# Magnitudes of two weights on VectorE, earlier and finer steps ahead of the first group, in a graph network kernel

## The chip, the core and the metric

The kernel runs on one core of one Trainium2 chip. A core has five engines with queues of their own: TensorE (PE in the profile, its weight loads PEld), VectorE (DVE), ScalarE (ACT), GpSimd (POOL) and SyncE (SP), which here only starts DMAs. They meet at semaphores: an instruction waits until a counter has a value, and its finished predecessor has raised it. The metric is the device time of one execution in microseconds; lower is better.

## The reference, cut to what matters

`x` is 64 x 128 x 512 (batch, channel, node). Everything is float32.

```python
def reference(x, adj, bias, W_lang, W_grav, W_V, W_O, gate_logit, log_sigma):
    # layer 0, over the 512 nodes, one graph for the whole batch
    xn = transpose(x, (2, 0, 1))                              # node, batch, channel
    x_norm = xn / maximum(norm(xn, axis=-1), 1e-12)
    mean_sim = einsum('nbl,mbl->nm', x_norm, x_norm) / B      # 512 x 512
    A = the 153 largest of each row of mean_sim without its own node, else 0
    dinv = where(A.sum(0) > 0, rsqrt(A.sum(0)), 0)
    An = dinv[:, None] * A * dinv[None, :]
    x = layernorm(x + transpose(einsum('sd,sbl->dbl', An, xn @ adj) + bias))
    # layer 1, a causal graph over the 128 channels of each batch item
    z_l, z_g, v = x @ W_lang.T, x @ W_grav.T, x @ W_V.T
    K_l = rows of max(cos(z_l, z_l), 0), causal, no diagonal, sum 1
    K_g = rows of exp(-dist2(z_g, z_g) / (2 sigma^2)), causal, no diagonal, sum 1
    K = w * K_l + (1 - w) * K_g                               # w = sigmoid(gate_logit)
    return layernorm(x + (K @ v) @ W_O.T)
```

## The kernel before

A float32 product is made of float16 parts: each operand is split into a high part (a cast) and a low part (the operand less its high part), and `three` (lines 263 to 267) multiplies high by high, high by low and low by high. So most tiles take a cast on ACT (a function named ..._high) and a subtraction on POOL or DVE (..._low). To keep the parts in range, each matrix is first scaled by a power of two from its largest magnitude, which the kernel reads from sums of squares.

The program has a prologue and a loop. The prologue takes about the first 190 us:

1. **Similarities.** `x` comes in 16 chunks (`NC`) of 4 rows (`CL`) each. For every chunk ACT squares, DVE sums and normalises (line 1445), ACT casts (L1009), POOL subtracts (L409, one instruction for each of the 4 rows, which raises `xn_l_ready`), and PE adds rows 0 and 1 of the 512 x 512 similarity matrix (`rows_01`, which waits for that row's `xn_l_ready`). After the last chunk PE makes rows 2 and 3 from the kept parts (`gram`), while the other engines work on rows 0 and 1.
2. **Magnitudes.** ACT squares the four weights and `adj` with a sum (L1048, L1072, L1074) into columns of `magn`. PE turns `magn` after chunk 4 of `gram`, DVE takes the maximum of each, ACT its root, PE spreads it after chunk 6 (L621), and DVE makes the scales (`scales`), which release ACT's scaling of the weights (L1085).
3. **The 153 nearest.** `pick` runs on DVE, for node rows 0 and 1 (pair 0) and then 2 and 3 (pair 1). It takes mean and deviation of a row (the root is ACT's, `deviation`), counts over three guessed thresholds, and takes the rest by maxima. Its count goes to PE (`needs_along`, L609), and its results (`keep`, L1640) are summed on PE (`degrees`, L909).
4. **Weight products.** Beside `pick`, PE multiplies W_V by W_O (`vo_product`), the first group's x by adj (`first_project`), and turns the other two weights (`turn_weight`, L644, with banks freed by ACT's `turned_low`, L1139) and multiplies each with itself (`upper_product`).
5. **The scaled graph** (L1701 to L1719) and **the first group**: `mix_nodes`, layernorm, `project_z`, and `project_group(1)`, which multiplies the second group's x by adj, into banks 0 to 3 that the z products before it have to leave first.

The loop then takes 16 groups of 4 batch items. Nothing in its body is changed; only the call for group 0 (in which the second group's x is projected) is.

Each engine runs its queue in the order in which the code is written, and the order was written by hand. Most tiles lie in one large SBUF tile, `arena`, so rows are told apart by their lines. Two more names: `first_x` is the first group's x, loaded when POOL has made the first low part (`w_l_ready` 1), and `xg[1]` is the second group's x.

## Time and profile before

| | us |
|---|---|
| median of 3 runs | 940.64 (940.01 to 943.67) |
| the profiled execution's own time | 940.67 |
| its span, first to last instruction | 938.90 |
| PE busy | 915.7 (98%) |
| DVE busy | 750.0 (80%) |
| ACT busy | 538.4 (57%) |
| POOL busy | 304.1 (32%) |

The profile lists every instruction of one execution with its start and length. In a timeline row stand the start, the time taken (of several merged instructions together), the engine, the line, the operation, out<-in, the shapes and the count, and in brackets how long the engine had been idle before it and what ended that. PE matmuls are pipelined, so starts are the better measure there. PEclk is the share of TensorE's full clock that was granted.

### The profile page before, as it was taken

How to read it: one execution, taken by the hardware profiler on the slowest of the kernel's cores; microseconds unless marked ns; L12 is line 12 of the kernel's file. 1: busy time of each engine (PE TensorE's matmuls, PEld its weight loads, DVE VectorE, ACT ScalarE, POOL GpSimd, SP SyncE). 2: the span in 40 equal slices, each digit the busy share in tenths (PEclk: the TensorE clock that was granted, in tenths of full speed). 3: DMA queues.
4: the chain of work that ended last, by engine and by line, in shares of the span. 5: the costliest groups of instructions: out<-in, count | busy, mean ns of one | idle time of the engine just before them, and what ended most of it. 6: DMA issues, size and time to landing. Idle time of an engine off the chain costs nothing.

```text
span 938.9 us, 18940 instructions
## 1 busy us (share of the span) xinstructions
PE 915.7 (98%) x6856; PEld 539.8 (57%) x6856; DVE 750.0 (80%) x1720; ACT 538.4 (57%) x984; POOL 304.1 (32%) x420
## 2 busy tenths in 40 slices
PE   8999998999999999999999999999999999999995
PEld 6777876565555464646464646454545454556452
DVE  5887588778887888888888888888888888887767
ACT  6987676676373646464646464646464646463623
POOL 5888262045050505050505050505050505050500
PEclk9999999999999999999999999999999999999998
DMA  8554121102323131313131313232323232321211
GB/s 307 190 196 148 60 91 45 46 2 44 103 49 100 37 109 37 108 37 108 38 108 38 107 38 107 39 106 39 106 39 106 40 105 40 107 43 59 45 46 45
DMA packets 100792, 75.58 MB, mean 80 GB/s; under 512 B 79504, under 2 KB 79632, under 8 KB 98832
## 3 DMA queue, kind: packets, MB, share of 16 engines
q1 hardware_dynamic: 100752, 75.05, 27.9%
q8 instruction: 24, 0.39, 0.2%
q14 instruction: 16, 0.13, 0.0%
HBM read 38.86 MB, written 16.78 MB: 59 GB/s over the span
## 4 chain that ended last, share of the span: by engine, by line
PE 63%; DVE 14%; ACT 4%; issue 3%; DMA 1%; POOL 1%; DVEq 0%; SPq 0%; ACTq 0%; POOLq 0%
PE bank L265 13%; PE bank L267 12%; PE bank L266 12%; PE pair L265 7%; PE pair L267 7%; PE pair L266 7%; DVE arena L1813 4%; DVE arena L1803 2%; DVE arena L1478 1%; ACT arena L1107 1%; PE bank L790 1%; ACT arena L1245 1%; PE bank L752 1%; PE bank L751 1%; DVE stats L1792 1%
## 5 line engine op out<-in xcount | busy, mean ns | idle before, releaser
L265 PE MATMUL bank<-arena 128*128 128x512 f16 (+2 forms) x1056 | 292.2, 301 | 4.1 <-DVE arena L1813 2.0
L266 PE MATMUL bank<-arena 128*128 128x512 f16 (+2 forms) x1056 | 291.8, 300 | 0.0
L267 PE MATMUL bank<-arena 128*128 128x512 f16 (+2 forms) x1056 | 291.8, 300 | 0.0
L265 PE MATMUL pair<-arena 128*128 128x512 f16 (+1 forms) x400 | 150.7, 377 | 0.0
L266 PE MATMUL pair<-arena 128*128 128x512 f16 (+1 forms) x400 | 150.4, 376 | 0.0
L267 PE MATMUL pair<-arena 128*128 128x512 f16 (+1 forms) x400 | 150.3, 376 | 0.0
L265 PEld LDWEIGHTS bank<-arena 128*128 128x128 f16 x1056 | 103.2, 98 | 66.0 <-DVE arena L1813 4.3
L267 PEld LDWEIGHTS bank<-arena 128*128 128x128 f16 x1056 | 103.3, 98 | 62.9
L266 PEld LDWEIGHTS bank<-arena 128*128 128x128 f16 x1056 | 103.3, 98 | 55.0 <-issue 0.7
L460 POOL TENSOR_TENSOR sq_parts<-cf,zero 128x4 bf16<-128x4 f32 x15 | 3.1, 208 | 373.9 <-DVE cf L1865 373.9
L1245 ACT ACTIVATE arena<-bank 128x512 f16<-128x512 f32 x64 | 37.5, 588 | 95.5 <-PE bank L267 95.5
L445 POOL TENSOR_TENSOR arena<-arena 128x512 f16<-128x512 f32 x60 | 69.4, 1156 | 54.8 <-ACT arena L1240 52.8
L441 POOL TENSOR_TENSOR arena<-arena 128x512 f32<-128x512 f32 x60 | 76.0, 1267 | 29.5 <-ACT arena L1122 29.0
L409 POOL TENSOR_TENSOR arena<-arena 128x512 f16<-128x512 f32 x64 | 72.8, 1160 | 21.0 <-ACT arena L1009 20.9
L267 PEld LDWEIGHTS pair<-arena 128*128 128x128 f16 x400 | 39.1, 98 | 46.3
L1813 DVE SCALAR_TENSOR_TENSOR arena<-bank,arena 128x512 f16<-128x512 f32 x64 | 43.9, 686 | 27.0 <-ACT arena L1245 27.0
L265 PEld LDWEIGHTS pair<-arena 128*128 128x128 f16 x400 | 39.0, 98 | 44.9
L266 PEld LDWEIGHTS pair<-arena 128*128 128x128 f16 x400 | 39.1, 98 | 42.4
L1235 ACT ACTIVATE arena<-arena,ln 128x512 f32<-128x512 f32 x64 | 51.3, 805 | 18.1 <-DVE ln L1782 18.1
L1250 ACT ACTIVATE arena<-bank 128x512 f16<-128x512 f32 x32 | 19.1, 596 | 68.6 <-PE bank L267 68.6
L1478 DVE SCALAR_TENSOR_TENSOR arena<-arena,up 128x512 f16<-128x512 f32 x60 | 43.8, 773 | 18.0 <-ACT arena L1107 18.0
L417 POOL TENSOR_TENSOR arena<-arena 128x256 f16<-128x256 f32 x45 | 30.9, 722 | 73.7 <-ACT arena L1153 34.1
(383 smaller groups left out, 1951.3 us busy)
## 6 DMA issues: line engine op xcount, KB each, us to landing
arena<-in_x SPq DMA_DIRECT2D x32, 1024.0 KB, 5.6
out_dram<-arena SPq DMA_DIRECT2D x15, 1024.0 KB, 4.3
arena<-arena SPq DMA_TRANSPOSE x74, 3.2
arena<-in_x SPq DMA_DIRECT2D x2, 512.0 KB, 4.5
arena<-in_w_grav_t SPq DMA_DIRECT2D x1, 1024.0 KB, 7.3
arena<-in_w_lang_t SPq DMA_DIRECT2D x1, 1024.0 KB, 5.4
arena<-in_w_v SPq DMA_DIRECT2D x1, 1024.0 KB, 8.4
arena<-in_w_o_t SPq DMA_DIRECT2D x1, 1024.0 KB, 9.3
```

The source lines that it names most:

```text
L265: pe.matmul(dst, ah, bh, start=start, stop=False)
L266: pe.matmul(dst, ah, bl, start=False, stop=False)
L267: return pe.matmul(dst, al, bh, start=False, stop=stop)
L409: pool.tensor_tensor(xn_l[:, c * CL + t, :], xc[c % SLOTS][:, t, :], xn_h[:, c * CL + t, :], ALU.subtract).then_inc(s["xn_l_ready"], 1)
L417: last = pool.tensor_tensor(dst[:, mine, :], raw[:, mine, :], hi[:, mine, :], ALU.subtract)
L441: pool.tensor_tensor(y[:, b, :], y[:, b, :], xg[slot][:, b, :], ALU.add).then_inc(s["y_ready"], 1)
L445: pool.tensor_tensor(h_l[:, b, :], h[slot][:, b, :], h_h[:, b, :], ALU.subtract).then_inc(s["hl_ready"], 1)
L1235: act.activation(h[slot][:, b, :], y[:, b, :], ACT.Identity, scale=ln1[:, 3, b:b + 1], bias=ln1[:, 4, b:b + 1]).then_inc(s["h_ready"], 1)
L1245: act.activation(z_h[i][:, E_ORDER[n], :, :], bank[n][:].rearrange("p (b n) -> p b n", b=GB), ACT.Copy, scale=U_DOWN).then_inc(done, 1)
L1250: act.activation(half_h[i], bank[4 + i][:].rearrange("p (b n) -> p b n", b=GB), ACT.Copy, scale=HALF_DOWN).then_inc(done, 1)
L1478: low = dve.scalar_tensor_tensor(x_l[:, b, :], xg[slot][:, b, :], up[:, 5:6], x_h[:, b, :], ALU.mult, ALU.subtract)
L1813: dve.scalar_tensor_tensor(z_l[i][:, e, :, :], bank[n][:].rearrange("p (b n) -> p b n", b=GB), U_DOWN, z_h[i][:, e, :, :], ALU.mult, ALU.s ...
```

## The change

- **Magnitudes.** ACT squares only weights 1 and 2; weights 0 and 3 are squared by DVE, with one multiply-and-sum instruction each, between the last normalisation and the filling of `work`. `adj` is squared right after the first two rows of S. PE turns `magn` after chunk 3 instead of 4 and spreads the roots after chunk 5 instead of 6.
- **Pair 0 of `pick`.** Each row is filled and its statistics are taken at once, instead of both rows first.
- **Rows 2 and 3 on PE.** Chunk 0 of `gram` is parted in two around `finish_diagonal(0)` and `(1)`. In the last chunk row 2 is finished ahead of row 3. `finish_diagonal(2)`, `(3)` and the turn of S go ahead of most of `turn_weight(1, 0)`, and ACT's `turned_high(1, 0)` goes behind S.
- **Finer subtractions.** POOL's low parts of weights 2 and 3, of the first x and of its product are made in pieces of 128 instead of 256.
- **Roots.** `deviation(1)` moves on ACT from behind `vo_out(0)` to behind the scaling of `first_x`; the degrees' root moves ahead of `upper_out(1, 2)`. On PE `needs_along(1)` goes into the middle of `vo_product(3)`, and the second half of `degrees` ahead of `upper_product(1, 2)`.
- **The second group's x.** Its cast and subtraction are made earlier, and PE projects it into banks 4 to 7.

```diff
+        squares_v = at(184 * KIB, [KB, NODES])
...
-                low(blocks(vo_l[i]), blocks(w_raw[2 + i]), blocks(vo_h[i]), 8, s["w_l_ready"])
+                low(blocks(vo_l[i]), blocks(w_raw[2 + i]), blocks(vo_h[i]), 16, s["w_l_ready"])
...
-            low(blocks(first_x_l), blocks(first_x), blocks(first_x_h), 8, s["x_l_ready"])
+            low(blocks(first_x_l), blocks(first_x), blocks(first_x_h), 16, s["x_l_ready"])
...
-                low(xw_l[:, b, :, :], first_xw[:, b, :, :], xw_h[:, b, :, :], 2, s["xw_l_ready"])
+                low(xw_l[:, b, :, :], first_xw[:, b, :, :], xw_h[:, b, :, :], KB, s["xw_l_ready"])
...
-            gram(0, range(2, KB), first=True)
+            gram(0, range(2, KB), first=True, ts=range(0, 2))
             finish_diagonal(0)
             finish_diagonal(1)
+            gram(0, range(2, KB), ts=range(2, CL))
...
-                gram(c, range(2, KB), last=(c == NC - 1))
-                if c == 4:
-                    pe.wait_ge(s["magn_ready"], 5)
-                    pe.wait_ge(s["magn_x"], 1)
+                if c < NC - 1:
+                    gram(c, range(2, KB))
+                else:
+                    gram(c, range(2, 3), last=True)
+                    gram(c, range(3, KB), last=True)
+                if c == 3:
+                    pe.wait_ge(s["magn_ready"], 3)
+                    pe.wait_ge(s["magn_x"], 3)
                     pe.transpose(bank[4][0:8, 0:P], magn[:], ident[:]).then_inc(s["magn_all_ready"], 1)
-                if c == 6:
+                if c == 5:
...
-            turn_weight(1, 0)
             finish_diagonal(2)
             finish_diagonal(3)
-            turn_weight(1, 1)
+            turn_weight(1, 0, range(0, 2))
             pe.wait_ge(s["S_ready"], 6)
             turn(bank[7][:, P:2 * P], 2, 3).then_inc(s["S_turned"], 1)
+            turn_weight(1, 0, range(2, KB))
+            turn_weight(1, 1)
...
-            def project_group(g):
+            def project_ahead(g):
                 pe.wait_ge(s["x_l_ready"], g + 1)
-                for b in range(GB):
-                    wait(pe, s["zg_l_ready"], g * GB - GB + (b + 1))
-                    project_x(g, b, x_h, x_l)
-
-            def project_ahead(g):
-
-                pe.wait_ge(s["x_l_ready"], g + 1)
-                pe.wait_ge(s["k_ready"], g - 1)
+                wait(pe, s["k_ready"], g - 1)
+                if isinstance(g, int) and g == 1:
+                    pe.wait_ge(s["u_out"], 2 * (2 * KB - 1))
...
-                    project_group(g + 1)
+                    project_ahead(g + 1)
...
-            vo_product(3)
+            vo_product(3, range(0, HALF))
             needs_along(1)
+            vo_product(3, range(HALF, KB))
             for b in range(GB):
                 first_project(b)
-            for d in range(KB):
-                upper_product(1, d)
+            upper_product(1, 0)
+            upper_product(1, 1)
             degrees(range(2, KB))
+            upper_product(1, 2)
+            upper_product(1, 3)
...
-            for n, i in enumerate((1, 0, 3)):
+            for n, i in enumerate((1, 2)):
                 act.wait_ge(s[f"w_in{i}"], 16)
                 wait(act, s["magn_ready"], n)
                 act.activation(squares, w_raw[i], ACT.Square, accum_out=magn[:, i:i + 1]).then_inc(s["magn_ready"], 1)
...
-            turned_high(1, 0)
...
+            turned_high(1, 0)
             turned_high(1, 1)
             act.wait_ge(s["w_in2"], 32)
             act.activation(first_x, first_x, ACT.Copy, scale=up[:, 5:6]).then_inc(s["w_scaled"], 1)
+            deviation(1)
...
             vo_out(0)
-            deviation(1)
...
+            x_high(1, 1, 1, range(0, 1))
             turned_low(0, 2)
             turned_low(0, 3)
+            x_high(1, 1, 1, range(1, HALF))
             first_roots(0, 0)
             first_norm(0, 0, 0)
             first_norm(0, 0, 1)
+            x_high(1, 1, 1, range(HALF, GB))
...
             upper_high(0)
-            x_high(1, 1, 1, range(GB))
...
             dve.tensor_reduce(magn[:, 5:6], chunk_max[:], AX.X, ALU.max).then_inc(s["magn_x"], 1)
+            dve.wait_ge(s["consts_made"], 4)
+            for n, i in enumerate((0, 3)):
+                dve.wait_ge(s[f"w_in{i}"], 16)
+                dve.wait_ge(s["magn_x"], n + 1)
+                dve.scalar_tensor_tensor(squares_v, w_raw[i], 1.0, w_raw[i], ALU.mult, ALU.mult,
+                                         accum_out=magn[:, i:i + 1]).then_inc(s["magn_x"], 1)
+            dve.wait_ge(s["magn_x"], 3)
             dve.wait_ge(s["xn_l_ready"], NC * CL)
             dve.memset(work[:, :, NODES:], PAD).then_inc(s["work_ready"], 1)
...
             for b in range(GB):
                 hT_low(b)
+            x_low(1, 1, range(GB))
```

What this makes of the queues is shown at three places. A row is an instruction with its line (the lines of the changed kernel lie a few further on), its operation, out<-in, the size of the output, what it waits for, and a count.

On DVE, at the end of the similarities, before:

```order
L1463 TENSOR_REDUCE magn<-chunk_max 128x1 [waits nrm_in]
L1465 MEMSET arena 128x4x8 [waits xn_l_ready]
L1470 COPY arena<-arena 128x512 [waits S_ready,consts_made]
L1472 TENSOR_TENSOR arena<-arena,self_mark 128x128 [waits work_ready]
L1470 COPY arena<-arena 128x512 [waits S_ready]
```

and now:

```order
L1470 TENSOR_REDUCE magn<-chunk_max 128x1 [waits nrm_in]
L1475 SCALAR_TENSOR_TENSOR arena,magn<-arena 128x2048 [waits magn_x,w_in0,consts_made]
L1475 SCALAR_TENSOR_TENSOR arena,magn<-arena 128x2048 [waits magn_x,w_in3]
L1479 MEMSET arena 128x4x8 [waits xn_l_ready,magn_x]
L1484 COPY arena<-arena 128x512 [waits S_ready,consts_made]
L1486 TENSOR_TENSOR arena<-arena,self_mark 128x128 [waits work_ready]
L1521 BN_STATS row_stats<-arena 128x6
```

Two instructions over 2048 elements each stand between the last reduction and the memset, and the statistics of row 0 stand ahead of the second copy.

On ACT, around the scaling of the first group's x (L1175, now L1178) and the root for pair 1 of `pick` (L1059, now L1067), before:

```order
L1135 ACTIVATE arena<-bank 128x512 [waits wn_ps]
L1175 ACTIVATE arena<-arena,up 128x2048 [waits w_in2]
L1178 ACTIVATE arena<-arena 128x2048 [waits w_l_ready,w_scaled]
L1139 ACTIVATE arena<-bank 128x512 [waits wn_rest] x2
L1157 ACTIVATE arena<-bank 128x512 [waits vo_ps]
L1159 ACTIVATE arena,vo_magn<-arena 128x512 [waits vo_out]
L1059 ACTIVATE guess<-guess 128x2 [waits var_ready]
```

and now:

```order
L1138 ACTIVATE arena<-bank 128x512 [waits wn_ps] x2
L1178 ACTIVATE arena<-arena,up 128x2048 [waits w_in2]
L1067 ACTIVATE guess<-guess 128x2 [waits var_ready]
L1182 ACTIVATE arena<-arena 128x2048 [waits w_l_ready,w_scaled]
L1142 ACTIVATE arena<-bank 128x512 [waits wn_rest] x2
L1160 ACTIVATE arena<-bank 128x512 [waits vo_ps]
```

The root stands four large instructions earlier, and the cast of the first x and `turned_low` (L1139, now L1142) stand behind it.

On ACT ahead of the first group, where `x_high` of the second group (L1107, now L1110) stood behind the last weight product's parts (L1153), before:

```order
L1153 ACTIVATE arena<-arena 128x1280 [waits u_out]
L1107 ACTIVATE arena<-arena,up 128x512 [waits xw_ps,x_in1]
L1107 ACTIVATE arena<-arena,up 128x512 x3
L1396 ACTIVATE arena<-arena,vo_scale 128x2048 [waits vo_steps]
L1245 ACTIVATE arena<-bank 128x512 [waits zg_ps] x2
```

and now:

```order
L1110 ACTIVATE arena<-arena,up 128x512 [waits xw_ps,x_in1]
L1142 ACTIVATE arena<-bank 128x512 [waits wn_rest] x2
L1110 ACTIVATE arena<-arena,up 128x512 [waits xw_ps,x_in1]
L1233 ACTIVATE ln<-ln 128x2 [waits ln1_var]
L1235 ACTIVATE ln<-ln 128x2 [waits ln1_log]
L1240 ACTIVATE arena<-arena,ln 128x512 [waits ln1_ready] x2
L1110 ACTIVATE arena<-arena,up 128x512 [waits xw_ps,x_in1]
L1110 ACTIVATE arena<-arena,up 128x512
```

The four casts are spread over the steps of the first layernorm, some 20 instructions earlier in the queue.

## Rows read from the trace of the kernel before

**Rows 1.** The page: busy time of each engine, its share, its instructions.

```profile
PE 915.7 (98%) x6856; PEld 539.8 (57%) x6856; DVE 750.0 (80%) x1720; ACT 538.4 (57%) x984; POOL 304.1 (32%) x420
```

**Rows 2.** Busy time by stretch: length, each engine's busy time, PEclk, DMA share, GB/s.

```profile
80.00:100.00 20.00, 20.00 (x162) 14.31 (x161) 11.82 (x21) 14.88 (x17) 17.36 (x16) 1.00 0.45 159
160.00:180.00 20.00, 18.73 (x96) 10.40 (x95) 16.97 (x47) 11.40 (x20) 0.00 (x0) 0.91 0.13 48
180.00:200.00 20.00, 18.73 (x149) 12.10 (x148) 13.74 (x31) 17.83 (x33) 5.00 (x6) 1.00 0.16 54
240.00:939.00 699.00, 684.67 (x4915) 374.13 (x4913) 565.73 (x1289) 366.88 (x711) 182.17 (x266) 0.99 0.26 68
```

**Rows 3.** Timeline of PE, the starts behind its waits in the prologue.

```profile
146.74 0.38 PE L609 MATMUL bank<-ident,guess 128*1 128x128 f32 x2 [0.82 <-DVE guess L1568]
...
157.36 1.95 PE L909 MATMUL bank<-ones,arena 128*128 128x1 f32 x16 [1.04 <-DVE arena L1640]
...
164.13 2.02 PE L644 MATMUL bank<-arena 128*128 128x128 f32 x16 [0.72 <-ACT arena L1139]
166.71 0.38 PE L265 MATMUL bank<-arena 128*128 128x512 f16 x1 [0.56 <-DVE arena L1719]
...
194.19 0.22 PE L265 MATMUL bank<-adj_h,arena 128*128 128x128 f16 x1 [1.26 <-DVE arena L1813]
```

**Rows 4.** Busy time by stretches of 2 us, columns as above.

```profile
156.00:158.00 2.00, 0.96 (x12) 0.78 (x9) 1.87 (x3) 1.44 (x3) 0.00 (x0) 1.00 0.00 0
...
160.00:162.00 2.00, 2.00 (x14) 2.00 (x13) 1.06 (x5) 0.85 (x2) 0.00 (x0) 0.63 0.96 362
162.00:164.00 2.00, 1.41 (x5) 0.40 (x3) 1.26 (x5) 2.00 (x4) 0.00 (x0) 0.52 0.28 106
```

**Rows 5.** Timeline of DVE at the end of the similarities.

```profile
92.70 2.35 DVE L1445 SCALAR_TENSOR_TENSOR arena<-arena,bank 128x1024 f32<-128x1024 f32 x2 [1.89 <-PE bank L513]
94.97 0.16 DVE L1463 TENSOR_REDUCE magn<-chunk_max 128x1 f32<-128x16 f32 x1
99.72 0.09 DVE L1465 MEMSET arena<- 128x32 f32 x1 [4.59 <-POOL arena L409]
```

**Rows 6.** Timeline of POOL, the low parts.

```profile
95.15 4.50 POOL L409 TENSOR_TENSOR arena<-arena 128x512 f16<-128x512 f32 x4 [0.37 <-ACT arena L1009]
...
118.71 11.09 POOL L417 TENSOR_TENSOR arena<-arena 128x256 f16<-128x256 f32 x16 [19.05 <-ACT arena L1087]
129.76 0.42 POOL L427 TENSOR_TENSOR adj_l<-adj_sb,adj_h 128x128 f16<-128x128 f32 x1
136.03 5.08 POOL L417 TENSOR_TENSOR arena<-arena 128x256 f16<-128x256 f32 x8 [5.84 <-ACT arena L1178]
...
188.35 4.54 POOL L417 TENSOR_TENSOR arena<-arena 128x256 f16<-128x256 f32 x5 [34.12 <-ACT arena L1153]
```

**Rows 7.** DVE groups by shape, 182 to 200 us: count, busy us, mean ns, idle before.

```profile
L1478 DVE SCALAR_TENSOR_TENSOR arena<-arena,up 128x512 f16<-128x512 f32 x4 | 4.4, 1168 | 2.6 <-ACT arena L1107 2.6
...
L1486 DVE SCALAR_TENSOR_TENSOR arena<-bank,arena 128x512 f16<-128x512 f32 x2 | 1.3, 682 | 0.0
```

**Rows 8.** Timeline of PE, the start of the last row of the last chunk.

```profile
99.71 0.23 PE L519 MATMUL bank<-arena 128*128 128x128 f16 x1
```

**Rows 9.** Timeline of ACT around the diagonal blocks and the first group's x.

```profile
102.19 0.42 ACT L1040 ACTIVATE rinv_rep<-bank 128x128 f32<-128x128 f32 x2
...
131.94 2.01 ACT L1175 ACTIVATE arena<-arena,up 128x2048 f32<-128x2048 f32 x1
134.04 1.91 ACT L1178 ACTIVATE arena<-arena 128x2048 f16<-128x2048 f32 x1
135.85 1.06 ACT L1139 ACTIVATE arena<-bank 128x512 f16<-128x512 f32 x2
```

**Rows 10.** Timeline of DVE, two waits in the chain of the nearest nodes.

```profile
113.99 0.17 DVE L1658 TENSOR_SCALAR pw<-bank 128x8 int32<-128x8 int32 x1 [0.40 <-PE bank L621]
...
138.29 0.32 DVE L1531 SCALAR_TENSOR_TENSOR guess<-guess 128x2 f32<-128x2 f32 x1 [2.14 <-ACT guess L1059]
```

More of the change, by code:

```diff
@@ L634, in project_x, with turn_weight @@
                 mm.then_inc(s["xw_ps"], 1)
-            def turn_weight(i, j):
+            def turn_weight(i, j, ks=range(KB)):
                 n = (1 - i) * KB + j
@@ L642, in turn_weight @@
                 wait(pe, s["wn_out"], n - 1)
-                for k in range(KB):
+                for k in ks:
                     mm = pe.matmul(bank[4 + j % 2][:, k * P:(k + 1) * P], w_raw[i][:, k, j * P:(j + 1) * P],
                                    ident_w[i], start=(k == 0), stop=(k == KB - 1), skip_group_check=True)
-                mm.then_inc(s["wn_ps"], 1)
-            turn_weight(1, 0)
+                if ks[-1] == KB - 1:
+                    mm.then_inc(s["wn_ps"], 1)
             finish_diagonal(2)
             finish_diagonal(3)
-            turn_weight(1, 1)
+            turn_weight(1, 0, range(0, 2))
             pe.wait_ge(s["S_ready"], 6)
             turn(bank[7][:, P:2 * P], 2, 3).then_inc(s["S_turned"], 1)
+            turn_weight(1, 0, range(2, KB))
+            turn_weight(1, 1)
             def first_project(b):
@@ L662, in _, with vo_product @@
             OUT_OF_ROW = [2, 4, 6, 7]
-            def vo_product(d):
+            def vo_product(d, fs=range(KB)):
                 pe.wait_ge(s["w_l_ready"], 2)
@@ L667, in vo_product @@
                     pe.wait_ge(s["S_ready"], 8)
-                for f in range(KB):
+                for f in fs:
                     mm = three(pe, bank[d][:], vo_h[0][:, f, d * P:(d + 1) * P], vo_l[0][:, f, d * P:(d + 1) * P],
                                vo_h[1][:, f, :], vo_l[1][:, f, :], start=(f == 0), stop=(f == KB - 1))
-                mm.then_inc(s["vo_ps"], 1)
+                if fs[-1] == KB - 1:
+                    mm.then_inc(s["vo_ps"], 1)
             def less_high(i, j):
@@ L819, in body @@
                 if isinstance(g, int) and g == 0:
-                    project_group(g + 1)
+                    project_ahead(g + 1)
                     pe.wait_ge(s["w_l_ready"], 4)
-                    project_z(g, slot, 0, (s["xw_l_ready"], g * GB + GB), s["zl_ps"])
-                else:
-                    project_z(g, slot, 0, (s["zg_l_ready"], g * GB), s["zl_ps"])
+                project_z(g, slot, 0, (s["zg_l_ready"], g * GB), s["zl_ps"])
                 pe.wait_ge(s["zg_l_ready"], g * GB + GB)
@@ L1051, in _ @@
             cross_out(1)
-            act.wait_ge(s["magn_ready"], 3)
+            act.wait_ge(s["magn_ready"], 2)
             act.wait_ge(s["xn_l_ready"], NC * CL)
@@ L1056, in _ @@
             s_out(S[:, 1, P:], bank[1][:, 0:NODES - P])
+            act.activation(squares2[:, 0, 0:P], adj_sb[:], ACT.Square,
+                           accum_out=magn[:, 4:5]).then_inc(s["magn_ready"], 1)
+            act.wait_ge(s["magn_x"], 3)
             def deviation(pair):
@@ L1070, in _ @@
             fill_out(work[:, 3, 0:2 * P], bank[6][:, 0:2 * P])
-            act.wait_ge(s["w_in2"], 16)
-            act.activation(squares2, w_raw[2], ACT.Square, accum_out=magn[:, 2:3]).then_inc(s["magn_ready"], 1)
-            act.wait_ge(s["magn_ready"], 4)
-            act.activation(squares2[:, 0, 0:P], adj_sb[:], ACT.Square,
-                           accum_out=magn[:, 4:5]).then_inc(s["magn_ready"], 1)
             deviation(0)
@@ L1200, in _ @@
             x_biased(slice(0, HALF))
-            for d in range(KB):
-                upper_out(1, d)
-            x_biased(slice(HALF, GB))
+            upper_out(1, 0)
+            upper_out(1, 1)
             act.wait_ge(s["deg_in"], 1)
             act.activation(deg_t[:], deg_m[:], ACT.Sqrt).then_inc(s["roots_made"], 1)
+            upper_out(1, 2)
+            upper_out(1, 3)
+            x_biased(slice(HALF, GB))
             turned_high(0, 0)
@@ L1260, in body @@
                 if not has_previous:
-                    xw_high(g + 1, 0)
+                    xw_high(g + 1, 4)
                 if isinstance(g, int) and g == 0:
@@ L1499, in pick @@
                 g = lambda i: guess[:, i, :]
-                if pair == 0:
-                    dve.wait_ge(s["work_ready"], 5)
-                else:
+                if pair == 1:
                     dve.wait_ge(s["work_23_ready"], 6)
@@ L1506, in pick @@
                 for t in range(2):
+                    if pair == 0:
+                        fill_work(t, 2 + t)
                     dve.bn_stats(row_stats[:, t, :], S[:, r0 + t, :]).then_inc(ps, 1)
@@ L1533, in pick @@
                 n += 2
+                dve.wait_ge(s["work_ready"], 5)
                 for i in range(COUNTS):
@@ L1643, in _ @@
             dve.wait_ge(s["consts_made"], 4)
-            fill_work(0, 2)
-            fill_work(1, 3)
             ss = s["scale_steps"]
@@ L1842, in body @@
                 if not has_previous:
-                    xw_low(g + 1, 0)
+                    xw_low(g + 1, 4)
                 if has_second and has_previous:
@@ L2114, in _ @@
             dve.wait_ge(cs, 10)
-            x_low(1, 1, range(GB))
             body(0, 0, True, False)
```

## The prediction

> **What bounds the kernel now.** I read the busy shares first: PE is busy for 98% of the span, 915.7 of 938.9 us [rows 1], so it is PE's queue that time has to leave, or enter. Next the stretches: from 240 us on PE is busy for 684.67 of 699 us [rows 2], and nothing in that loop is changed. So the change can win only what PE idles in the prologue, and lose whatever it makes PE wait there. Third, the starts on PE that follow a wait, up to 200 us [rows 3]: 0.82 us for the count of pair 1 (L609), 1.04 for the last kept rows (L909), 0.72 for a freed bank (L644), 0.56 for the scaled graph (L265 behind L1719), 1.26 for the second group's x. These sum to 4.4 us; with the pipeline's tail, which these rows count as busy, each gap between two matmuls is some 0.2 us wider, say 5.4 in all. Last the clock: 1.00, but for 160 to 164 us, where 0.63 and 0.52 were granted [rows 4], so TensorE ran for about 3.4 us at the lower of its levels, 1.2 GHz. Ahead of that it had idled, and then run 16 matmuls one column wide in 1.95 us [rows 3].
>
> At the end of the similarities there is next to nothing to win: PE is busy for 20.00 of 20 us from 80 to 100 [rows 2]. What matters is who feeds it. POOL makes the last four low parts in 4.50 us from 95.15, 1.12 us each, without a pause [rows 6], the last ends at 99.65, and PE starts on it at 99.71 [rows 8]. POOL is the pace there, with no slack. DVE idles beside it from 95.13 to 99.72 [rows 5].
>
> **Squares on DVE: what they cost.** The two new instructions take 2048 elements each. L1445 takes 1.17 us for 1024 elements [rows 5], so one is 2.25 us and two are 4.5. On DVE alone they fit: they would end just before or a little behind 99.72, and DVE has nothing until S, 5 us later. But they read two operands from SBUF, as L1445 does not (its second comes from PSUM). What such an instruction does beside POOL is seen at 189 us: L1478, with both inputs in `arena`, takes 1168 ns, where L1486, of the same size but with one input in a bank, takes 682 [rows 7]. POOL pays at the same time: its five pieces there take 4.54 us, 0.91 each, against 5.08 for eight, 0.63 each, at 136 us [rows 6]. (4.54 - 5 x 0.63 = 1.4 us, for the two to three DVE instructions of 0.6 us that fell between.) So the engines take turns, an instruction of one, then one of the other, and each waits for the whole of the other's.
>
> Put at 95 us: POOL starts its first part at 95.15, just ahead of DVE, and ends at 96.27. DVE's first square runs to 98.45, POOL's second part to 99.55, DVE's second square to 101.8, POOL's third and fourth to 102.9 and 104.0. The last low part comes 4.3 us late. If DVE is first by a hair, the sum is the same. PE takes the four parts in steps of 1.04 us, so it waits 2.0 us for the second, 2.2 for the third, and starts the last at 104.0 in place of 99.7: **+4.3 us**, all on the path. From below, the cost is 0, if an instruction that reads the same tile twice does not meet POOL, or waits until POOL has finished. From above it is 4.5.
>
> The Trainium skill, "SBUF — State Buffer", section "Who interferes with whom", says that a DVE instruction with two SBUF inputs contends with a GpSimd one that reads SBUF, and that whoever starts first holds the shared port pair for the whole instruction. The trace agrees at 512 elements (1168 against 682 ns); that it holds over 2048 no row shows. By this rule the change loses here, as above.
>
> **The clock.** Between 97.6 and 102.9 us PE would have 1.04 us of work in 5.3. That is emptier than the stretch which came before the low clock at 160 us [rows 4]. I expect one period of 3.4 us at 1.2 GHz, as there, beginning some 4.4 us after the emptiness sets in (160.6 less 156.2), so at 102 and to 105.4. PE would have 2.5 us of it to work, and loses half: **+1.2 us**. Bounds: 0, and 3.4 for two full periods.
>
> **Magnitudes and pair 0.** ACT's three squares held up its copies of the diagonal blocks until 102.19 [rows 9]; without the third, and with chunk 0 parted, PE saves about 0.2 us. DVE gets the deviation of pair 0 some 0.8 us sooner (one row's statistics are taken while S is turned) and no longer waits 0.40 us for the spread roots [rows 10], so weights are scaled 1.2 us sooner. PE's turns of `magn` cost nothing, they only stand 1.6 us earlier. But then DVE waits for `needs_along(0)`, whose place on PE stays: of 1.2 us about 0.6 to 0.9 is left at the start of pair 1.
>
> **Finer subtractions.** 128 elements take 0.42 us alone (L427), 256 take 0.63, 512 take 1.12 [rows 6]; in a row I take 0.39. Sixteen are 6.2 us where eight were 5.08. DVE waits less for each; together POOL ends the two weights at about 131, 1.2 us later, and `vo_product(0)`, due at 130.9, waits some 0.3 us.
>
> **Roots, and the chain to the graph.** The deviation of pair 1 waited 2.14 us behind ACT's four instructions [rows 10]. Now ACT scales `first_x` until about 133.7, then stands until DVE has the variance at about 135.4 (136.15 before, less 0.75). DVE goes on at 135.7 in place of 138.29, **2.6 us sooner**, and with it the count and the kept rows. The price is on ACT: the cast of `first_x`, at 134.04 before, starts at 135.6, and `turned_low` ends its first tile at 138.1 in place of 136.4 [rows 9]. `turn_weight(1, 2)` needs that bank and is due at about 137.0: PE waits 1.0 to 1.3 us there, where it hardly waited. This takes the place of the 1.0 us at L609, which goes. The 1.2 us gap ahead of L909 goes too, since `degrees` finds its rows done at 155.3. DVE then gets the degrees at about 157.0 (159.34 before), but PE spreads the result only after both turns of weight 0, at 160.6 in place of 161.50. From there all is as before, at the higher clock: the graph's first tile, and with it `mix_nodes` (166.71), comes **1.15 us sooner** [rows 3]. Bounds: 0, if ACT's stand at the root grows by a microsecond, and 2.5, if it vanishes.
>
> **The second group's x.** Its four casts fall into idle stretches of ACT, and its low parts come before POOL begins the next ones. At 192.8 us PE goes straight on into banks 4 to 7: the gap ahead of 194.19 goes, 1.26 us in the row and 1.43 between matmuls [rows 3]: **-1.4 us**. What is next late, the parts of z for `project_z(0)`, is due 2.7 us later and done by then.
>
> **Sum.** +4.3 + 1.2 - 0.2 - 1.15 - 1.4 = +2.75 us. The profiled execution took 940.67, 0.03 from the median of 940.64, with 1.8 us around its span that nothing changes. 940.67 + 2.75 = **943.4 us**.
>
> **Rivals.**
> - *A: the squares cost nothing on POOL.* Then the clock's term goes too: -2.75, 937.9 us. For it: no row shows one tile read twice, nor 2048 elements. Against it: L1478 [rows 7].
> - *B: POOL is held up, but the clock stays at the higher level.* +4.3 - 2.75 = +1.55, 942.2 us. For it: PE idled for 1 us and more elsewhere (146, 194 us) with no lower clock. Against it: no such stretch there is as empty.
> - *C: the delay at the similarities brings two periods at 1.2 GHz, and ACT's stand at the root eats the gain on the graph.* It is still the squares that decide, with the low clock falling on full work: +4.3 + 3.4 - 1.6 = +6.1, 946.8 us. It decides from 3.2 us of clock loss on, with the rest as forecast.
> - *D: no hold-up, and the chain to the graph gains its upper bound:* -2.75 - 1.35 = -4.1, 936.5; faster by more than 0.5% only if the freed clock at 160 us also gives its whole microsecond back.
>
> **Chances.** Forecast 0.42, B 0.20, A 0.14, C 0.18, D 0.06. A measurement of this kernel can tell about 0.5%, 4.7 us, from no change: below 935.9 is faster, above 945.3 slower. That gives slower 0.20 (C and a little of the forecast's upper end), faster 0.06, the same 0.74. The forecast alone has 942 to 945. To hold 8 in 10 the range takes in A and the lower half of C: 937.5 to 946.0.
>
> **What would show it.** Right: the two DVE instructions at 95 to 102 us take well over 2.3 us each by the profile, or POOL's L409 there does; PE's last row starts near 104; PEclk falls below 1 within 100 to 106; DVE's wait for the root of pair 1 is under 0.4 us; PE waits about 1 us on L644 behind `turned_low` near 138 (all plus 4 to 5 us); no wait is left ahead of the second group's projection. Wrong, and then A: POOL's four parts still take 4.5 us and PE's last row starts by 100. The step most likely to fail is the hold-up, then the clock.

## The result, and the profile after

The changed kernel takes **945.51 us** (median of 8 executions, 943.95 to 949.37), the kernel before 940.85 in the same session (8, 940.01 to 943.67): ratio **1.005, 95% interval 1.0034 to 1.0066**, some 4.7 us slower. Run again later (*e12*), beside 23 executions of the kernel before, it took 944.57 us (6, 944.35 to 945.43) against 941.57, ratio 1.0038 [1.0026, 1.005]. Forecast were 943.4 us and a range of 937.5 to 946.0. In *e4*, *e9* and *e10* below one execution each took 1.3, 1.09 and 2.3 ms; the medians hold it, the ratios leave it out. The profiled execution took 944.26 us, 3.6 more than that of before. Line numbers are those of each kernel: L409 of before is L410 after, L417 is L418, L265 is L266, L644 is L650.

The page of the kernel after, its span and its busy row (PE 1.0 us busier than in [rows 1], in a span 3.6 us longer):

```profile
span 942.5 us, 18980 instructions
PE 916.7 (97%) x6856; PEld 540.0 (57%) x6856; DVE 753.3 (80%) x1724; ACT 535.0 (57%) x980; POOL 313.3 (33%) x452
```

The end of the similarities, timelines of POOL and of DVE, to be read against [rows 5, 6]:

```profile
95.27 8.59 POOL L410 TENSOR_TENSOR arena<-arena 128x512 f16<-128x512 f32 x4 [0.37 <-ACT arena L1014]
```

```profile
95.39 3.19 DVE L1475 SCALAR_TENSOR_TENSOR arena<-arena 128x2048 f32<-128x2048 f32 x1
...
98.69 3.05 DVE L1475 SCALAR_TENSOR_TENSOR arena<-arena 128x2048 f32<-128x2048 f32 x1
...
104.01 0.09 DVE L1479 MEMSET arena<- 128x32 f32 x1 [2.26 <-POOL arena L410]
```

POOL's four parts take 8.59 us where they took 4.50. Both squares are recorded with more than 3 us, where the same instructions take 2.29 us without POOL beside them (*e1* below). That fits a record which begins while the instruction still stands for its turn. The timeline of PE there, against [rows 8]:

```profile
97.60 0.27 PE L542 MATMUL bank<-arena 128*128 128x256 f16 x1
99.65 0.23 PE L520 MATMUL bank<-arena 128*128 128x128 f16 x1 [1.78 <-POOL arena L410]
...
100.59 0.27 PE L542 MATMUL bank<-arena 128*128 128x256 f16 x1
102.81 0.23 PE L520 MATMUL bank<-arena 128*128 128x128 f16 x1 [1.95 <-POOL arena L410]
```

The two waits show when POOL's second and third parts were done, just ahead of 99.65 and 102.81: 3.2 us apart, one part of 1.1 and one square of 2.2. These steps are those of engines that take turns by whole instructions. Busy time by stretches of 2 us (length, PE, PEld, DVE, ACT, POOL, then PEclk, DMA share, GB/s), first behind the waits, then at the place of [rows 4]:

```profile
101.00:103.00 2.00, 0.19 (x2) 0.17 (x3) 0.75 (x2) 0.00 (x0) 2.00 (x2) 1.00 0.00 0
103.00:105.00 2.00, 2.00 (x10) 1.09 (x8) 0.09 (x1) 0.00 (x0) 0.87 (x1) 0.52 0.00 0
105.00:107.00 2.00, 2.00 (x14) 1.27 (x13) 0.00 (x0) 0.52 (x2) 0.00 (x0) 0.63 0.00 0
```

```profile
160.00:162.00 2.00, 2.00 (x20) 1.84 (x18) 1.04 (x2) 1.15 (x5) 2.00 (x4) 1.00 0.00 0
162.00:164.00 2.00, 2.00 (x26) 1.86 (x27) 1.38 (x8) 0.62 (x3) 0.86 (x3) 1.00 0.79 236
```

The lower level (1.2 GHz) lay at 160 us before, and lies at 103 to 106.6 now, right behind the two waits. The starts on PE behind a wait from there on, against [rows 3], and the wait of DVE for the root of pair 1, against [rows 10]:

```profile
137.09 0.39 PE L266 MATMUL bank<-arena 128*128 128x512 f16 x1 [0.29 <-POOL arena L418]
...
143.60 0.57 PE L650 MATMUL bank<-arena 128*128 128x128 f32 x3 [0.73 <-ACT arena L1142]
...
168.48 2.02 PE L650 MATMUL bank<-arena 128*128 128x128 f32 x16 [1.34 <-ACT arena L1142]
...
240.22 0.39 PE L266 MATMUL bank<-arena 128*128 128x512 f16 x1 [0.56 <-DMA arena<-arena]
```

```profile
141.21 0.16 DVE L1545 SCALAR_TENSOR_TENSOR guess<-guess 128x2 f32<-128x2 f32 x1 [0.27 <-ACT guess L1067]
```

The waits at the count of pair 1, at the last kept rows and at the second group's x are gone, that at the start of `mix_nodes` is 0.14 us (0.56 before); one at L650 near 143 us and one for a transposing DMA at 240 us are new.

How much later than before each place is reached tells where the time went. PE's turns of S: +5.56 us. The start of `mix_nodes`: 170.64 for 166.71, +3.93. The second group's x: +2.50. What starts at 256 us before, in the third group: +3.52. The last instructions: +3.62.

### The profile page after: what moved, and what is told of

Read it like the earlier page. It is cut to its first block, busy times and chain, and to the rows that moved or that the text cites. A ratio compares the mean times of both kernels' runs of the same rounds, so it can differ in the third digit from the quotient of the medians.

```text
span 942.5 us, 18980 instructions
## 1 busy us (share of the span) xinstructions
PE 916.7 (97%) x6856; PEld 540.0 (57%) x6856; DVE 753.3 (80%) x1724; ACT 535.0 (57%) x980; POOL 313.3 (33%) x452
## 4 chain that ended last, share of the span: by engine, by line
PE 64%; DVE 13%; ACT 3%; issue 3%; DMA 1%; POOL 1%; SPq 1%; DVEq 0%; ACTq 0%; POOLq 0%
PE bank L266 13%; PE bank L268 12%; PE bank L267 12%; PE pair L266 7%; PE pair L268 7%; PE pair L267 7%; DVE arena L1825 4%; DVE arena L1815 2%; PE bank L794 1%; DVE arena L1492 1%; ACT arena L1110 1%; ACT arena L1250 1%; DMA arena<-arena 1%; PE bank L756 1%; PE bank L755 1%
## 5 line engine op out<-in xcount | busy, mean ns | idle before, releaser
L266 PE MATMUL bank<-arena 128*128 128x512 f16 (+2 forms) x1056 | 292.2, 300 | 4.9 <-DVE arena L1825 3.0
L266 PE MATMUL pair<-arena 128*128 128x512 f16 (+1 forms) x400 | 150.7, 377 | 0.0
L266 PEld LDWEIGHTS bank<-arena 128*128 128x128 f16 x1056 | 103.2, 98 | 67.3 <-DVE arena L1825 5.3
L446 POOL TENSOR_TENSOR arena<-arena 128x512 f16<-128x512 f32 x60 | 69.4, 1156 | 54.8 <-ACT arena L1245 52.8
L410 POOL TENSOR_TENSOR arena<-arena 128x512 f16<-128x512 f32 x64 | 76.9, 1224 | 21.1 <-ACT arena L1014 21.0
L266 PEld LDWEIGHTS pair<-arena 128*128 128x128 f16 x400 | 39.1, 98 | 44.8
L418 POOL TENSOR_TENSOR arena<-arena 128x128 f16<-128x128 f32 (+1 forms) x77 | 35.5, 497 | 66.9 <-ACT arena L1156 29.4
```

Of the source, the lines that this page charges most:

```text
L266: pe.matmul(dst, ah, bh, start=start, stop=False)
L410: pool.tensor_tensor(xn_l[:, c * CL + t, :], xc[c % SLOTS][:, t, :], xn_h[:, c * CL + t, :], ALU.subtract).then_inc(s["xn_l_ready"], 1)
L418: last = pool.tensor_tensor(dst[:, mine, :], raw[:, mine, :], hi[:, mine, :], ALU.subtract)
L446: pool.tensor_tensor(h_l[:, b, :], h[slot][:, b, :], h_h[:, b, :], ALU.subtract).then_inc(s["hl_ready"], 1)
```

## The experiments

Each has 5 to 12 executions and a ratio to the kernel before, run on the same chip in the same session. There were three sessions on three chips: *e1* to *e4*, *e5* to *e8*, *e9* to *e12*. Between two of them the ratios are the measure, not the medians.

One more number helps to read them, the mean granted clock of an execution. It holds the end of the program, where PE has nothing left to do and the lower level is granted in every profile, for 5 to 7 us:

```profile
936.00:942.00 6.00, 0.00 (x0) 0.00 (x0) 3.13 (x10) 1.84 (x4) 0.00 (x0) 0.50 0.46 175
```

A stretch of 3.4 us at half the clock takes another 0.0018 off the mean over 940 us. So it is in the fourteen profiles: 0.996 or 0.997 without such a stretch ahead of PE's last matmul, 0.994 or 0.995 with one, 0.993 with two or with one of 6.6 us.

**e3 and e4: the disputed cost alone.** The kernel before with two added DVE multiplies of 2048 elements, whose result nobody uses, where the change puts its squares; PE's turn of S waits for them. They differ in the second input alone.

```diff
+            for n, i in enumerate((0, 3)):
...
+                dve.scalar_tensor_tensor(squares_v, w_raw[i], 1.0, w_raw[i], ...)                  # e3
+                dve.scalar_tensor_tensor(squares_v, w_raw[i], 1.0, <bank 6, broadcast>, ...)       # e4
```

> The kernel before, with two added multiplies of 128x2048 on DVE that nothing uses, at the place of the new squares, both inputs from SBUF (a weight twice), and a wait of PE's turns of S on them. Theory: POOL's four L409 take 8.6 us, PE's last row starts at 104, a low clock follows, and the time is 940.85 + 4.3 + 1.2 = 946.3. Rival (any long DVE instruction there, or the waits, costs): the same for this run, but then the run with a PSUM operand must show it too.

> As the run before, but the second input of the two added multiplies is a bank of PSUM, repeated over the four blocks; the product is not used. Theory: DVE and POOL run side by side, 4.5 us for POOL's four parts, 940.8 to 941.1. Rival (length or the waits cost, not the second input): 945 or more. If DVE is slower with PSUM as an input, its two instructions end by 100.5 at the latest and nothing waits for them.

*e3*: 947.59 us, ratio 1.0073 [1.0058, 1.0088], 1.3 us more than forecast. *e4*: 941.36, 1.0005 [0.9994, 1.0015]. POOL and DVE in *e3*, then in *e4*:

```profile
95.19 8.59 POOL L410 TENSOR_TENSOR arena<-arena 128x512 f16<-128x512 f32 x4 [0.36 <-ACT arena L1011]
...
95.28 3.21 DVE L1469 SCALAR_TENSOR_TENSOR arena<-arena 128x2048 f32<-128x2048 f32 x1
```

```profile
95.15 4.52 POOL L410 TENSOR_TENSOR arena<-arena 128x512 f16<-128x512 f32 x4 [0.36 <-ACT arena L1011]
...
95.24 2.29 DVE L1469 SCALAR_TENSOR_TENSOR arena<-arena,bank 128x2048 f32<-128x2048 f32 x1
98.83 2.29 DVE L1469 SCALAR_TENSOR_TENSOR arena<-arena,bank 128x2048 f32<-128x2048 f32 x1 [1.30 <-DMA arena<-in_w_o_t]
```

Same place, same size, and the same starts (the second multiply stands for its weight's load and starts at 98.83 us here, at 98.75 in *e3*): with both inputs in SBUF, here one tile read twice, POOL loses 4.1 us and PE's turns of S come 5.5 us late; with one of them in a bank neither engine loses anything. This settles the mechanism. *e3* also shows a second stretch at 1.2 GHz, near where before has its own. It falls on fuller work: the start of `mix_nodes` is 6.2 us late, not 5.5. Stretches of *e3*, then of *e4*:

```profile
100.00:110.00 10.00, 8.05 (x71) 5.94 (x69) 1.74 (x2) 3.53 (x8) 3.79 (x2) 0.83 0.01 2
160.00:170.00 10.00, 8.30 (x61) 7.34 (x58) 5.80 (x21) 4.62 (x11) 0.00 (x0) 0.83 0.34 107
```

```profile
160.00:170.00 10.00, 8.25 (x52) 5.29 (x52) 8.73 (x22) 8.28 (x14) 0.00 (x0) 1.00 0.25 94
```

*e4* has the waits of before at the same places (0.83 us at 146.75, 1.05 at 157.38) and no low clock behind them; its `mix_nodes` starts 0.63 us sooner than before. So the stretch at 160 us belongs to the profiled execution and not to the kernel: of 87 further executions of the kernel before 33 have a mean of 0.996 or 0.997, which no profile with such a stretch has. Why it comes in some and not in others stays open.

**e1: the squares held back.** The changed kernel, with DVE's wait for POOL's last part ahead of the squares and not behind them.

```diff
             dve.wait_ge(s["consts_made"], 4)
+            dve.wait_ge(s["xn_l_ready"], NC * CL)
             for n, i in enumerate((0, 3)):
...
-            dve.wait_ge(s["xn_l_ready"], NC * CL)
```

> The changed kernel with one edit: DVE waits for POOL's last low part (xn_l_ready 64) before its two squares instead of behind them. Theory (two SBUF inputs hold POOL up): POOL's four parts are back at 4.5 us, PE starts its last row at 99.8, no low clock within 100 to 107 us, and the squares take 2.2 us each, so that they end at about 104.2 and the filling of work starts 0.3 us late. Time: 944.3 less 4.3 and 1.2 is 938.8, at most 939.3. Rival (the loss is elsewhere in the change, in the cast order or in the finer pieces): 944 or more, with the lines of POOL unchanged.

938.79 us (11, 937.21 to 940.62), ratio 0.9977 [0.9967, 0.9986]: one wait moved makes a kernel some 6 us faster than the changed one (0.9977 against 1.005 and 1.0038), and faster than the one before. The theory held. POOL's four parts take 4.51 us, the squares 2.29 each, PE has no wait there and no low clock at 103 us.

**e9: one square early, the other held back.** The changed kernel with DVE's wait for POOL's last part between the two squares.

> The changed kernel with its first square where the change put it, beside POOL's four subtractions, and only the second held back until POOL is done. Theory (POOL loses time in proportion to the time that DVE squares beside it: 4.1 us lost beside 6.2 us of squares in the changed kernel): one square of about 3.1 us costs POOL 2.0 us, POOL's parts take 6.5 us and not 8.6, PE waits about 2 us once, and without the second wait the low clock of 102 to 107 us does not come: 940.8 us. Rival (the low clock comes from any late row of chunks there): 942.

940.56 us, 0.9999 [0.9987, 1.0012]. POOL's four parts, and PE behind its one wait:

```profile
95.18 6.55 POOL L410 TENSOR_TENSOR arena<-arena 128x512 f16<-128x512 f32 x4 [0.37 <-ACT arena L1014]
```

```profile
99.55 0.23 PE L520 MATMUL bank<-arena 128*128 128x128 f16 x1 [1.77 <-POOL arena L410]
```

Half the squares, half the loss (2.05 of 4.1 us), and PEclk is 1.00 as long as PE works: one wait of 2 us did not bring the low clock, two within 5 us did, in *e3* as in both profiles of the changed kernel. The executions agree: 9 of 11 in *e9* have a mean clock of 0.996 or 0.997, none of the 14 of the changed kernel or the 5 of *e3* has. The theory held, the rival fell.

**e2 and e10: the magnitudes' part.** *e2* is the changed kernel with this part as before; *e10* the kernel before with this part alone and the squares held back.

> The changed kernel with the magnitudes as before: ACT squares all four weights at their old places, PE turns magn after chunk 4 and spreads the roots after chunk 6; the other edits stay. Theory: no hold-up, no low clock at 100 us; scales come 0.4 to 1.2 us later than in the run with late squares, which the chain of pair 1 feels by 0.3 to 0.8: 939.0 to 940.0. Rival: 944 or more.

> The kernel before with the magnitudes' part of the change alone (two weights squared by DVE, held back until POOL is done; magnitudes turned behind chunk 3 and 5), none of the other parts. Undoing this part in the changed kernel gave 941.6 us, against 938.8 with it and the squares held back. Theory (the part is worth something by itself, since ACT comes 1 to 2 us sooner to what DVE and PE wait for): 0.5 to 2 us faster than before, 939.5 to 940.5. Rival (it pays only together with the deviation taken sooner, which without it stands in front of ACT's other work): no difference, 941.

*e2*: 941.63, 1.0012 [0.9995, 1.003], 2.8 us above *e1* and above its own forecast; its executions are spread from 938.92 to 946.35. By the profiles, which both have a stretch at 1.2 GHz at 16 to 20 us, PE's last matmul comes 2.3 us later than in *e1*. *e10*: 941.54, 0.9996 [0.9984, 1.0007]: nothing, as its rival had it. In *e2* ACT squares until 103.8 us and PE waits 0.97 us for its copies of the diagonal blocks; DVE comes later to the variance of pair 1, and ACT, which since the change stands for it ahead of its other work, stands 3.03 us and not 1.67 (*e1*). In *e10* DVE waits 2.65 us for the root, which still lies behind ACT's other work:

```profile
138.68 0.31 DVE L1537 SCALAR_TENSOR_TENSOR guess<-guess 128x2 f32<-128x2 f32 x1 [2.65 <-ACT guess L1063]
```

Together they say: what DVE gains early is only passed on if the root is early too, and an early root is only cheap if DVE is early.

**e5 and e6: where ACT takes the deviation of pair 1**, both on *e1*.

```diff
-            deviation(1)
             act.wait_ge(s["w_scaled"], 3)
             act.wait_ge(s["w_l_ready"], 2)
             act.activation(first_x_h, first_x, ACT.Copy).then_inc(s["x_h_ready"], GB)
+            deviation(1)          # e5
             turned_low(1, 0)
             turned_low(1, 1)
             vo_out(0)
+            deviation(1)          # e6
```

> The kernel with the squares held back until POOL's last part (938.8 us, ratio 0.998 to the kernel before), and in it one more edit: ACT takes the second half's deviation behind the rounding of first_x and not ahead of it. In that kernel ACT stands 1.67 us for DVE's variance with the rounding, two halves of turned weights and the first vo product behind it, and PE waits 0.90 us at turn_weight(1, 2). Theory (ACT's stand is what PE waits for): the rounding fills the stand, ACT comes to the halves of the weights 1.5 us sooner, PE's 0.90 us wait goes, DVE goes on 0.2 us later, and the end comes 0.7 to 0.9 us sooner: about 938.0 us. Rival (the graph's chain decides, PE's wait costs nothing): the wait goes but comes back at the degrees or at mix_nodes, and the time stays at 938.8.

> The same kernel as the one before it, with the second half's deviation where the kernel before had it, behind the first vo product on ACT: DVE goes on about 2.4 us later (ACT at 139.4 and not at 136.9). Theory (the graph's chain is what the earlier deviation bought): the 0.90 us wait at turn_weight(1, 2) goes, but the waits at the needed rows (1.0 before) and at the degrees (1.2 before) come back, so the kernel is 0.5 to 1.2 us slower than with the deviation ahead: 939.3 to 940.0. Rival (the chain has slack of its own by now): no wait comes back, 0.9 us faster, 937.9.

*e5*: 940.21, 0.9986 [0.9976, 0.9997]. *e6*: 942.46, 1.0005 [0.9993, 1.0017], over 2 us above its theory's range. In *e5* the 0.90 us between matmuls at `turn_weight(1, 2)` goes and 1.07 us comes at the degrees (first row); in *e6* 1.54 us comes at the count (second fence) and 1.46 at the degrees, and with them, in the profiled execution, 6.6 us at 1.2 GHz from 158 us on:

```profile
155.16 1.95 PE L911 MATMUL bank<-ones,arena 128*128 128x1 f32 x16 [0.90 <-DVE arena L1655]
```

```profile
146.33 0.38 PE L611 MATMUL bank<-ident,guess 128*1 128x128 f32 x2 [1.37 <-DVE guess L1583]
```

So DVE's chain bounds here, and the wait at L650 only covers it: the rival of *e5* held. The root's new place is worth 2.6 us beside the other edits by the ratios (*e6* less *e1*; 3.7 by the medians of two chips), and part of it is clock. Four of the twelve executions of *e6* have a mean clock of 0.996 or 0.997; they take 939.99 to 940.65 us, where the five such ones of *e5* take 938.71 to 939.16. So the waits cost some 1.2 us against *e5*, and in the other eight a low clock comes on top.

**e7 and e8: the second x and the piece size undone**, both on *e1*.

> The kernel with the squares held back, and in it the second group's x undone: high and low parts at the end of the prologue, its product into banks 0 to 3 as these come free. Theory (the prediction's term of -1.4 us is right and stays to the end): PE waits 1.4 us again at the second group's x near 191 us, and everything behind is 1.4 us later: 940.2. Rival (part of it was given back at once: in the changed kernel 1.0 us of the gain went again at the second group's transposing DMA, which took 2.57 us and not 1.23): the end is only 0.4 us later, 939.2.

> The kernel with the squares held back, and in it POOL's subtractions in pieces of the size of before: 256 and 512 elements in place of 128. POOL's row took 0.39 us a piece of 128 and 0.63 us a piece of 256, so each of the two weights is done 1.2 us sooner. Theory (finer pieces are a cost): PE's 0.52 us wait for POOL at the first vo product goes, the end is 0.3 to 0.5 us sooner, about 938.4. Rival (finer pieces let DVE in sooner, and the graph's chain is late without them): DVE's selection ends later by some tenths, PE's waits at the degrees come back, and the time is 0.5 us or more longer, 939.3.

*e7*: 939.70, 0.998 [0.997, 0.9989]. The wait is back:

```profile
192.83 0.22 PE L266 MATMUL bank<-adj_h,arena 128*128 128x128 f16 x1 [1.26 <-DVE arena L1830]
```

Counted from the turns of S, *e7* stands 1.4 us behind *e1* at the second group's x, 1.9 at the third group and 1.3 at PE's last matmul. So the profiles have the term to the end; the executions can't tell it from the rival's 0.4, since the ratios are 0.0003 (0.3 us) apart and the medians 0.9 us, with overlapping intervals. *e8*: 940.86, 0.9993 [0.9981, 1.0004], 1.5 us above *e1* by the ratios, 2 by the medians, also with overlapping intervals. PE's wait for POOL is gone, but DVE's instructions beside POOL are longer, *e8* and then *e1*:

```profile
125.97 1.30 DVE L1635 TENSOR_SCALAR cut<-rank,guess 128x8 f32<-128x8 f32 x2
```

```profile
127.66 0.62 DVE L1635 TENSOR_SCALAR cut<-rank,guess 128x8 f32<-128x8 f32 x2
```

Without POOL beside them these two take 0.36 us. A piece of 256 makes each wait up to 0.63 us, one of 128 up to 0.39. Finer pieces cost POOL 2.7 us over both weights (13.82 for 11.09), yet counted from the turns of S the start of `mix_nodes` comes 0.9 us sooner with them, and PE's last matmul 1.3. So the rival held by the profile; by the executions it is likely, not shown.

**e11: the end of the chain in another order**, on *e1*.

```diff
+            <PE: wait for dinv, four transposes into bank 6>
             turn_weight(0, 0)
             turn_weight(0, 1)
-            <the same>
...
+            x_biased(slice(HALF, GB))
             upper_out(1, 2)
             upper_out(1, 3)
-            x_biased(slice(HALF, GB))
+            upper_high(1)
             turned_high(0, 0)
             turned_high(0, 1)
-            upper_high(1)
```

> The kernel with the squares held back (938.8 us), and in it the end of the graph's chain in another order: PE broadcasts the inverse roots right behind the upper products and ahead of two turned weights (which stood 1.8 us in front of it), ACT biases the second half of x in its idle time behind the degrees' root and takes the upper weight's high part ahead of the turned ones. Theory: DVE's scaling of the adjacency starts 1.7 us sooner, PE's wait of 1.52 us at turn_weight(0, 2) shrinks to about 0.9, mix_nodes starts 0.6 to 1.0 us sooner, and the end comes with it: 938.0. Rival (ACT's turned halves are late for the weights, since they have the upper part ahead of them): nothing gained, 938.8 or more.

**937.20 us** (6, 936.20 to 938.85), ratio **0.996 [0.9947, 0.9973]**, the fastest of all. The profiles of *e1* and *e11* are not in step (that of *e1* has a stretch at 1.2 GHz at 16 to 20 us), so dates are counted from PE's turns of S, at 106.52 and 104.81 us. DVE's scaling of the graph starts 57.76 us behind them in *e1* and 56.06 in *e11*, 1.70 sooner; `mix_nodes` 60.05 and 59.10, 0.95 sooner; the end 1.2 sooner. PE's 1.52 us ahead of `turn_weight(0, 2)` is 0.36, with 0.64 ahead of the second L684. By the profiles the theory held; the two ratio intervals, those of *e1* and *e11*, still overlap. Timeline of PE in *e11*:

```profile
158.34 0.66 PE L939 MATMUL bank<-ident,rinv_rep 128*128 128x128 f32 x4
...
162.05 2.02 PE L650 MATMUL bank<-arena 128*128 128x128 f32 x16 [0.19 <-ACT arena L1141]
```

**e12: the changed kernel again.**

> The changed kernel unchanged, beside the others on one chip, for the spread of its times: eight runs lay between 943.95 and 949.37 us, their mean granted clock between 0.995 and 0.991. Theory (each further stretch at the lower clock, as the kernel before has one at 160 us, costs 1.5 to 2.5 us, and the spread is nothing else): the times fall with the clock on the same steps, near 944 at 0.995 and near 946.5 at 0.993, and a run at 0.997 does not occur, since the stretch at 103 us is always there. Rival (the spread has another cause): times of one clock spread as far as all of them.

Its six times lie at 944.35 to 944.99 with a mean clock of 0.995 or 0.994 and at 945.43 with 0.993. In the first session 0.995 gave 943.95 to 944.33, 0.993 gave 945.45 to 946.70, 0.991 gave 949.23 and 949.37. No execution had more than 0.995. The theory held in the main: none reaches 0.996, and the times go by the clock, 0.994 with 0.995 (the end of the program makes that difference) and 0.993 above them, though in *e12* 1 us below the 946.5 forecast for it. By the profiles a step of 0.002 is one more stretch at 1.2 GHz. What it costs depends on what PE had to do in it: 1.6 us at 103 us (below), 0.6 at `mix_nodes` and 0.3 at the end for the one at 160 us (before against *e4*). Which stretches came in the slowest two no profile shows.

## Why the prediction was nearly right, and where not

The sum against the trace of the profiled execution, each term as the shift that appears at its place:

| term | predicted | measured |
|---|---|---|
| hold-up of POOL | +4.3 | +4.21, its last part done at 103.86 for 99.65 |
| the clock behind it | +1.2 | +1.59 |
| diagonal blocks | -0.2 | -0.24, so +5.56 at the turns of S |
| the graph's chain | -1.15 | -1.63 up to `mix_nodes` |
| second group's x | -1.4 | -1.43 |
| groups behind it | 0 | +1.12 |
| sum | +2.75 | +3.62 |

The diagonal blocks' term is read from *e8* and *e11*, which have neither hold-up nor an early low clock and whose turns of S start at 104.81 us (105.05 before); the clock is what is left of the 5.56. Two terms were too small by 1.5 us together (clock, groups), and the others erred by 0.65 the other way. That the forecast lies only 0.9 us from the profiled execution is in part luck. The first median of 945.51 lies past the 945.3 from which on the prediction called the result slower, with a chance of 0.20; that of *e12*, 944.57, does not.

- **Squares.** Right in each date: PE's waits 1.94 and 2.11 us between matmuls (2.0 and 2.2 forecast), DVE's second square done at 101.7 (101.8), PE's last row from 104.58 (104.0), since the clock was low by then. *e3* against *e4* shows the cause. Rival A is refuted. The trace agrees with the rule of the Trainium skill that the prediction weighed ("SBUF — State Buffer", "Who interferes with whom"), now at 2048 elements too, where no row of before showed it.
- **Clock.** Right in kind, one stretch of 3.4 us, 103.2 to 106.6 for 102 to 105.4, but under-sized: 1.59 us for 1.2. The prediction gave PE 2.5 us of work in the stretch; it began behind the second wait, so PE had work in all of it. *e9* removes one wait and the stretch with it: POOL's last part is done 2.08 us late (101.73), the turns of S are 1.83 late, and the difference is the diagonal blocks' gain, with no clock in it. Rival B is refuted for this kernel.
- **Not foreseen at the clock:** the stretch at 160 us of before goes in the profiled execution, but five of the first eight executions had a clock one or two steps lower than it, so the first median lies 1.2 us above the profiled execution; that of *e12* lies only 0.2 above its own. Whether the further stretches came at the similarities, as rival C had it, no profile shows. Nor did the prediction ask whether the stretch at 160 us is there in every execution of before; *e4* says that it isn't.
- **Magnitudes.** PE's turns of `magn` cost nothing, as forecast. That DVE's lead is mostly lost at `needs_along(0)` is right too; *e10* shows that alone it is worth nothing.
- **Finer subtractions.** Forecast 0.3 us at `vo_product(0)`, measured 0.29 of waiting, 0.46 between matmuls; 6.2 us for sixteen pieces, measured 6.21. The sign of the whole was missed: "DVE waits less for each" was given no number, and *e8* shows it to weigh at least as much.
- **Roots.** DVE's wait at the root is 0.27 us (under 0.4 forecast); PE waits 0.90 us between matmuls behind `turned_low` (1.0 to 1.3), L609 and L909 find their rows ready. The chain's gain was 0.5 us larger than forecast, and 0.63 of its 1.63 us is the stretch at 160 us that falls away (before against *e4*): without it the chain gained 1.0. The wait at L650 near 168 grew from 1.14 to 1.52 us between matmuls, where the prediction had "all as before": ACT's biasing of x now stands ahead of the turned weights. *e11* moves that among other things, so its share alone is argued and not shown.
- **The failed step: "from 240 us on ... nothing in that loop is changed", so a shift passes through it as it is.** It does not. In the second group one DMA transpose (L328) takes 2.57 us where it took 1.23 (SP's queue, below), PE waits 0.72 us between matmuls for it at 240.22 and 0.58 at 256.44 (0.33 before); at 288 us part of it comes back (0.68, where before waited 1.39), and then up to 0.1 us is lost in each group, up to +3.62. *e7* has 0.69 and 0.59 there without the second x's edit, so that edit is not what takes it; *e1*, *e5*, *e9* and *e11* lose 0.3 to 1.1 us behind the second group, *e6* and *e12* 1.4, *e3* and *e4*, built on the kernel before, 0.3, and *e10*, built on it too, none. The transpose is not all of it: in *e11* it takes 1.23 us as before, with no wait at 240 us, and 0.4 us is lost. Why the loop meets its DMAs differently with the change's order stays open; no experiment isolated it.

```profile
232.90 2.57 SPq L328 DMA_TRANSPOSE arena<-arena  x1
```

## What to carry to other kernels

Ask of an "idle" engine what its new work shares with its neighbour. Here a DVE instruction with both inputs in SBUF held POOL up for nearly its whole length (2.05 us for one of 2.29), so beside a POOL row that feeds PE it cost about its own time on the path; put it behind the row, or read one input from PSUM. Moves along one chain pay together or not at all: follow each queue that the moved instruction now stands in front of, and test the parts in combination. If PE waits twice in a few microseconds, look at the granted clock behind it. And look at the mean clock of every execution before you take a gap from one profile: a stretch of before need not be a property of the kernel.

## What was unexpected in the hardware

- The same tile as both inputs counts as two: 8.59 us of POOL against 4.52 with a bank as the second (*e3*, *e4*).
- Small instructions are held up by POOL too: L1635, with 8 elements of one tile and a scalar column as inputs, two in 0.36 us alone, 0.62 beside pieces of 128, 1.30 beside pieces of 256 (*e1*, *e8*).
- One wait of 1.9 us on PE left the clock at 2.4 GHz (*e9*); two, 1.0 us of work apart, brought 3.4 us at 1.2 GHz (changed kernel, *e3*).
- The same waits near 160 us came with 3.4 us at 1.2 GHz behind them in one execution (before) and with none in another (*e4*).
